# A four-layer transformer kernel: the second layer's bands, rotary tables and normalisation set in another order

## Chip, cores and metric

One core of one Trainium2 chip. The metric is the device time of one execution in microseconds. The kernel before took 1456.38 us, the median of three runs (1453.41 to 1458.69).

## What is computed

Eight blocks of 128 tokens by 512 values (x) pass through four layers of cross-attention and feed-forward; each sub-layer adds to x what it computes from the layer-normalised x. The change lies between the first feed-forward (L0F) and the second (L1F). The part of the reference that it touches:

```python
# L0 ffn: router softmax over 8 heads, low-rank A and B
scores = H * softmax(x @ Wr.T + br); low = einsum('bsd,hrd->bshr', x, A)
out = 2 * einsum('bshr,hor,bsh->bso', low, B, scores)
# L1 xattn: the 76 of 128 channels that are largest in the context are "crucial"
crucial, sub = mask * x, (1 - mask) * x
c = [max(crucial, ch), mean(crucial, ch)]; s = [max(sub, ch), mean(sub, ch)]
A1, A2 = (sigmoid(relu(batch_norm(conv1d(v, conv_w, pad=3)))) for v in (c, s))
x = x + crucial * A1 + sub * A2
# L1 ffn: top-2 router, low-rank pair, base product
x = x + ffn(layernorm(x))
# L3 xattn needs rotary tables: cos_t[position_ids], sin_t[position_ids]
# and k = ctx @ Wk (8 heads), v = ctx @ Wv
```

## The kernel before, in words

Every engine's work is written out by hand as one queue for each engine, in the functions under `block.sync` (SP, the loads and stores), `block.gpsimd` (POOL), `block.scalar` (ACT), `block.vector` (DVE) and the one of TensorE (PE); semaphores alone tie the queues together, so the order in which a queue is written is the order in which it waits. `link` (an instruction, then a wait of the same engine for it) is used where an engine reads what it has just written.

Float32 products run as three passes of a high and a low half (`mm3`, L413, L417, L418). Weights come in 137 units of 128x512: SP loads a unit into `stage` (5 places), ScalarE rounds it into `ring_h` (L1213), GpSimd writes the rest into `ring_l` (L1036), both rings have 10 places. `hi.upto(n)` and `lo.upto(n)` run these steps up to unit n, `load.upto(n)` the loads.

**Context pieces.** The keys and values of the fourth layer are 32 pieces of 12 products each (`kv_pe`, evicted by ScalarE in `kv_act`, L814, stored by SP). They depend on the context only and are strewn between other work as filler for TensorE. Piece i waits for the eviction of piece i - 2.

**Router 0** (`router_pe`, `router_act`, `router_dve` with i = 0). TensorE makes the logits and the low-rank product, turns the logits (L727), VectorE adds the bias and subtracts the maximum (L628 to L632), ScalarE takes exp (L600), VectorE weights `low` (L651); TensorE meanwhile runs pieces 0 to 3 and turns `low` (L755); VectorE multiplies (L658) and splits (L663). GpSimd at that time makes the low half of the context, `cTl` (L1084), 1024 wide.

**Masks loop** (L1690 to L1698). VectorE normalises the eight blocks into `xnf` (L464), TensorE transposes each (L2129), VectorE multiplies with the mask and takes maxima, ScalarE takes the sums (L1376). Transposes of block b wait for the masks of block b - 2. Pieces 6, 7 and 8 follow blocks 3, 5 and 7.

**Rotary tables.** For each quarter q of the tokens GpSimd writes a one-hot matrix of the positions (`one_hot`, L1093), TensorE multiplies the tables with it (`tables_pe`, L2117), ScalarE copies cosine and sine out (L1362). One-hot q waits for product q - 1. Quarter 0 is done before the masks loop, 1 to 3 after it, with pieces 9, 10 and 11 between.

**Bands and the chain** (L1699 to L1729). The convolution over channels is a product with six banded matrices, which VectorE builds from the 14 taps (`band`, L608 to L622: one shift matrix, then 6 chains of tensor_scalar and scalar_tensor_tensor) after the masks loop. TensorE then does 24 matmul records (L2144), VectorE, TensorE (two totals, L2148), GpSimd (square root, L1107, L1108) and ScalarE (exp, L1391) take turns, and VectorE has the gains. Piece 12 follows the totals.

**Factor loop** (L1731 to L1748). For each block VectorE makes the channel factors `gT` from mask and gains (L1737), TensorE transposes them (L2156), VectorE multiplies with `xnf` (L1746), adds to X (L1747) and takes statistics (`ln_step`, L432, L435). Pieces 13 to 17 follow blocks 1 to 5. After the loop the layer norm of L1F runs over all eight blocks: `ln_dve` (normalise L464, low half L479), `ln_pe` (transposes L497), `ln_act` (high half L517), with pieces 18 to 20; then router 1, whose low-rank product starts on TensorE at 390.23 us.

## Time and profile before

| | us |
|---|---|
| median of three runs | 1456.38 (1453.41 to 1458.69) |
| the profiled execution's own time | 1461.52 |
| its span, first to last instruction | 1459.7 |
| PE busy | 1322.6 (91%) |
| DVE busy | 959.1 (66%) |
| ACT busy | 594.0 (41%) |
| POOL busy | 548.5 (38%) |

A profile is one execution. Busy times of different engines overlap. The timeline gives, for each instruction or run of like ones (xN), its start from the span's start, the time it took, and in brackets how long the engine stood idle before it and what ended that. The windows view sums the same records over a stretch and adds the clock that TensorE was granted (1.00 is full speed, 0.50 half).

### The profile page before, as it was taken

The page shows a single profiled execution, that of the slowest core. Times are in us where ns is not written, and L with a number is a line of the kernel's source. Part 1 is how long each engine was busy: PE and PEld are TensorE (multiplying, and loading weights), DVE is VectorE, ACT ScalarE, POOL GpSimd, SP SyncE. Part 2 cuts the span into 40 slices and gives each one's busy share as a digit, 9 for nine tenths or more (in the row PEclk, how much of TensorE's full clock was granted, in tenths as well). Part 3 has the DMA queues.
Part 4 walks back from the last instruction along what each step waited for, and adds up shares of the span by engine and source line. Part 5 has one row for each costly group of instructions (what it writes and reads, how often), then busy time and mean ns, then how long its engine had stood idle before and what let it go on. Part 6 is the DMA issues. An engine that isn't in the chain of part 4 may idle for free.

```text
span 1459.7 us, 20660 instructions
## 1 busy us (share of the span) xinstructions
PE 1322.6 (91%) x6958; PEld 996.1 (68%) x6958; DVE 959.1 (66%) x2109; ACT 594.0 (41%) x1614; POOL 548.5 (38%) x548
## 2 busy tenths in 40 slices
PE   2888877988899999999999899999999999999797
PEld 1555544767677777677878777777777777777565
DVE  6999956596633688843222566777777777677745
ACT  2777773361312344433121324344343444344341
POOL 5001003642313444142221444464554645445274
PEclk9999887998999999999999999999999999999999
DMA  5211111211221000031110131011111111110001
GB/s 168 59 30 43 31 25 63 87 66 65 73 80 51 1 8 30 1 95 51 38 56 23 51 100 52 30 58 51 37 58 59 58 41 46 51 37 30 1 1 58
DMA packets 53610, 71.68 MB, mean 49 GB/s; under 512 B 5936, under 2 KB 24689, under 8 KB 53507
## 3 DMA queue, kind: packets, MB, share of 16 engines
q1 hardware_dynamic: 52592, 69.15, 15.0%
q10 hardware_dynamic: 914, 1.22, 0.3%
q8 instruction: 57, 0.93, 0.3%
q14 instruction: 47, 0.38, 0.1%
HBM read 55.67 MB, written 10.49 MB: 45 GB/s over the span
## 4 chain that ended last, share of the span: by engine, by line
PE 63%; DVE 17%; issue 7%; POOL 6%; ACT 4%; DMA 2%; SPq 1%; POOLq 0%; DVEq 0%; ACTq 0%
PE bank L413 15%; PE bank L418 14%; PE bank L417 14%; PE bank L2399 3%; DVE topv L1603 2%; PE bank L2279 2%; PE bank L2375 2%; POOL ring_l L1036 2%; PE bank L2261 2%; DVE top L1597 2%; PE bank L2386 1%; DVE bank L1883 1%; DVE xn L1863 1%; DVE xn L1849 1%; POOL probs L1183 1%
## 5 line engine op out<-in xcount | busy, mean ns | idle before, releaser
L1036 POOL TENSOR_TENSOR ring_l<-stage,ring_h 128x512 fp32r<-128x512 f32 x137 | 181.9, 1346 | 250.5 <-ACT ring_h L1213 250.5
L413 PE MATMUL bank<-xTh_b,ring_h 128*128 128x512 f32 x464 | 189.9, 409 | 4.4 <-issue 3.0
L417 PE MATMUL bank<-xTl_b,ring_h 128*128 128x512 f32 x464 | 184.3, 397 | 0.0
L418 PE MATMUL bank<-xTh_b,ring_l 128*128 128x512 f32 x464 | 184.3, 397 | 0.0
L1158 POOL TENSOR_TENSOR q<-xn 128x512 f32<-128x512 f32 x64 | 82.6, 1291 | 205.6 <-DVE xn L1863 205.6
L413 PE MATMUL bank<-ring_h,o3h 128*128 128x512 f32 x256 | 125.3, 490 | 3.5 <-issue 3.5
L1507 ACT ACTIVATE probsT<-bank 128x512 f32<-128x512 f32 x64 | 38.2, 598 | 203.4 <-PE bank L2386 203.4
L1519 ACT ACTIVATE probs<-bank,nbias 128x128 f32<-128x128 f32 x256 | 90.5, 366 | 51.0 <-DVE nbias L1885 51.0
L413 PEld LDWEIGHTS bank<-xTh_b,ring_h 128*128 128x128 f32 x464 | 88.0, 190 | 25.0 <-issue 6.4
L418 PEld LDWEIGHTS bank<-xTh_b,ring_l 128*128 128x128 f32 x464 | 87.7, 189 | 21.5
L418 PE MATMUL bank<-ring_h,o3l 128*128 128x512 f32 x256 | 101.6, 397 | 0.0
L417 PE MATMUL bank<-ring_l,o3h 128*128 128x512 f32 x256 | 100.6, 393 | 0.0
L417 PEld LDWEIGHTS bank<-xTl_b,ring_h 128*128 128x128 f32 x464 | 88.0, 190 | 18.3
L1863 DVE TENSOR_TENSOR xn<-bank,sinT 64x512 f32<-64x512 f32 x128 | 88.1, 688 | 1.7
L1213 ACT ACTIVATE ring_h<-stage 128x512 fp32r<-128x512 f32 x137 | 81.8, 630 | 17.2 <-DMA stage<-in_units_dram 16.9
L1895 DVE TENSOR_TENSOR o3l<-bank,o3h 128x512 fp32r<-128x512 f32 x64 | 44.3, 692 | 58.3 <-ACT o3h L1529 58.3
L1877 DVE TENSOR_TENSOR X<-X,bank 128x512 f32<-128x512 f32 x64 | 44.0, 687 | 52.2 <-PE bank L418 51.8
L1814 DVE TENSOR_TENSOR hid<-silu,bank 128x512 f32<-128x512 f32 x22 | 15.1, 688 | 93.9 <-PE bank L418 86.3
L2375 PEld LDWEIGHTS bank<-k,q 128*128 128x128 f32 x512 | 67.7, 193 | 7.0 <-issue 1.7
L1183 POOL TENSOR_TENSOR probs<-probs,rsums 128x512 f32<-128x512 f32 x64 | 66.6, 1040 | 15.4 <-DVE rsums L1891 15.4
L2399 PE MATMUL bank<-probsT,v 128*128 128x512 f32 x128 | 67.2, 606 | 4.8 <-ACT probsT L1507 4.8
L2375 PE MATMUL bank<-k,q 128*128 128x128 f32 x512 | 68.3, 277 | 0.3 <-POOL q L1158 0.3
(332 smaller groups left out, 3249.4 us busy)
## 6 DMA issues: line engine op xcount, KB each, us to landing
stage<-in_units_dram SPq DMA_DIRECT2D x137, 256.0 KB, 3.0
ring_l<-k SPq DMA_DIRECT2D x64, 64.0 KB, 2.1
raw_k<-kvs SPq DMA_DIRECT2D x16, 256.0 KB, 2.1
kraw<-raw_k SPq DMA_DIRECT2D x16, 256.0 KB, 3.5
v<-raw_v SPq DMA_DIRECT2D x16, 256.0 KB, 2.8
stage<-in_context_dram SPq DMA_DIRECT2D x8, 256.0 KB, 2.9
raw_v<-kvs SPq DMA_DIRECT2D x8, 256.0 KB, 2.0
out_dram<-X SPq DMA_DIRECT2D x8, 256.0 KB, 2.0
```

The source lines that it names most:

```text
L413: ins = nc.tensor.matmul(out_ap, wh, mh, start=start, stop=False)
L417: nc.tensor.matmul(out_ap, wh, ml, start=False, stop=False)
L418: return nc.tensor.matmul(out_ap, wl, mh, start=False, stop=stop)
L1036: nc.gpsimd.tensor_tensor(ring_l[:, place_of(u), :], stage[:, u % STAGE, :], f32(ring_h[:, place_of(u), :]), ALU.subtract).then_inc(w_lo, 1)
L1158: nc.gpsimd.tensor_tensor(dst, xn[:, (at - 1) % 2, :], xn[:, 2 + (at - 1) % 2, :], ALU.add).then_inc(a3_ad, 1)
L1183: nc.gpsimd.tensor_tensor(pb, pb, rsums[:, n % 4, :].unsqueeze(2).to_broadcast((P, 4, P)), ALU.mult).then_inc(a3_pn, 1)
L1213: nc.scalar.activation(ring_h[:, place_of(u), :], stage[:, u % STAGE, :], ACT.Copy).then_inc(w_hi, 1)
L1519: ins = nc.scalar.activation(probs[:, n % 3, c], bank[n % 2][:, c], ACT.Exp, bias=nbias[:, n % 4, r:r + 1], scale=-1.0, accum_out=psums[:, ...
L1863: ins = nc.vector.tensor_tensor(xn[to, 2 + i % 2, :], src[fro, :], sinT[to, c], ALU.mult)
L1895: nc.vector.tensor_tensor(o3l[:, m % 2, :], bank[3 + m % 2][:], f32(o3h[:, m % 2, :]), ALU.subtract).then_inc(a3_ol, 1)
L2375: ins = nc.tensor.matmul(bank[n % 2][:, r * P:(r + 1) * P], q3[:, r, c], k3[:, c], start=True, stop=True)
L2399: nc.tensor.matmul(bank[3 + m % 2][:], v3[:, m % 8, :], probsT[:, m % 3, :], start=True, stop=True).then_inc(a3_pv, 1)
```

## The change

- `band` for the bands 0 to 2 is called in `router_dve` (i = 0) ahead of the wait for the turned logits, for 3 to 5 behind the weighting of `low`; the call after the masks loop goes.
- Rotary tables: cosine and sine (64 rows each) are one 128-row table, so a quarter's product has half the matmuls. `tables_pe(1)` moves behind block 1's transposes in the masks loop, `tables_pe(2)` behind block 5's, `tables_pe(3)` behind piece 9. ScalarE copies per half of the tokens, four copies of 64 rows each, the first half of the sine negated, after its sums.
- Pieces 6, 7 and 8 follow blocks 2, 4 and 6 of the masks loop; pieces 10 and 11 the two totals; 12 to 17 blocks 2 to 7 of the factor loop; 18 to 20 come after it. Pieces 12 to 17 use banks 4 and 5 instead of 6 and 7; piece 12 waits for ScalarE's second table copy.
- The layer norm of L1F is made block by block in the factor loop: statistics at once (`ln_one`), normalising one round later, transposes after the piece of round b + 2, the low half three rounds later. GpSimd takes the square roots in `ln_root`, with the low parts of units 12 and 13 between.
- GpSimd's one-hot 2 comes before unit 8's low part. SP loads one unit further ahead from piece 8 on.
- `xnf` is multiplied in place, `gT` lies in `probs` and `probsT`, both totals in one bank. VectorE still makes the channel factors, four instructions a block.

In the order of the file (the tables' constants and the buffers are left out):

```diff
-        tabs = probsT[:, 0:2, :].rearrange("p a (k j) -> p a k j", k=KT)
+        tabs = probsT[:, 0, :].rearrange("p (k j) -> p k j", k=KT)
+        gT = (probs[:, 2, :], probsT[:, 2, :])
...
+            if i == 0:
+                for k in range(3):
+                    band(v, k)
...
+            if i == 0:
+                for k in range(3, 6):
+                    band(v, k)
...
+                if i == 12:
+                    t.wait_ge(su_rc, 2)
...
-        def router_pe(t, i, n_ln, u, th, tl):
-
-            def between(b):
-
-                if b == 3:
-                    kv_pe(t, 21)
-                if b == 5:
-                    router_logits_pe(t, i, 0, th, tl)
-
-            if i == 1:
-                kv_pe(t, 20)
-                ln_pe(t, n_ln, between)
+        def router_pe(t, i, u, th, tl):
+
-            if i == 1:
-                t.wait_ge(c_ev, 21)
...
-            first = 0 if i < 4 else 6 if i < 18 else 4 if i < 24 else 0
+            first = 0 if i < 4 else 6 if i < 12 else 4 if i < 24 else 0
...
-            nc.sync.dma_start(tabs, d["tabs"].rearrange("a k p j -> p a k j")).then_inc(s_rest, 16)
+            nc.sync.dma_start(tabs, d["tabs"].rearrange("k p j -> p k j")).then_inc(s_rest, 16)
-                load.upto(unit_kv(i) + (10 if i >= 18 else 5))
+                load.upto(unit_kv(i) + (10 if i >= 18 else 6 if i >= 8 else 5))
...
+            one_hot(2)
-            one_hot(2)
-            lo.upto(U_L1F)
-            ln_pool(g, LN_L1F[0])
+            lo.upto(12)
+            for b in range(B):
+                ln_root(g, LN_L1F[0], b)
+                if b < 2:
+                    lo.upto(13 + b)
...
-            def tables(q):
-
-                a.wait_ge(su_rope, q + 1)
-                for i in range(2):
-                    ins = nc.scalar.activation((cosT, sinT)[i][:, q * 256:(q + 1) * 256], bank[5 - 3 * (q % 2)][:, i * 256:(i + 1) * 256],
-                                               ACT.Copy)
-                ins.then_inc(su_rc, 1)
-
-            tables(0)
+            def tables(half):
+
+                a.wait_ge(su_rope, 2 * half + 2)
+                c = slice(half * HALF, (half + 1) * HALF)
+                low_rows, high_rows = slice(0, 64), slice(64, P)
+                for to in (low_rows, high_rows):
+                    nc.scalar.activation(cosT[to, c], bank[5 - half][low_rows, :], ACT.Copy)
+                nc.scalar.activation(sinT[low_rows, c], bank[5 - half][high_rows, :], ACT.Copy, scale=-1.0)
+                nc.scalar.activation(sinT[high_rows, c], bank[5 - half][high_rows, :], ACT.Copy).then_inc(su_rc, 1)
+
...
-                if b in (3, 5, 7):
-                    kv_act(a, 6 + (b - 1) // 2)
-                if b in (4, 6):
-                    hi.upto(7 + b // 2)
+                if b in (2, 4, 6):
+                    kv_act(a, 6 + b // 2)
+                if b in (3, 5):
+                    hi.upto(9 + b // 5)
+            kv_act(a, 10)
+            tables(0)
-            kv_act(a, 10)
-            tables(2)
-            kv_act(a, 11)
-            tables(3)
-            kv_act(a, 12)
-            hi.upto(11)
+            hi.upto(12)
-            kv_act(a, 13)
-            hi.upto(12)
-            kv_act(a, 15)
-            hi.upto(U_L1F)
-            kv_act(a, 18)
+            kv_act(a, 12)
+            for b in range(B):
+                if b < 2:
+                    hi.upto(13 + b)
+                else:
+                    kv_act(a, 11 + b)
+                    ln_act(a, LN_L1F[1], xTh_a, b - 1, b - 2)
+            kv_act(a, 19)
+            ln_act(a, LN_L1F[1], xTh_a, 7, 6)
+            hi.upto(U_L1F + 1)
+            kv_act(a, 20)
+            ln_act(a, LN_L1F[1], xTh_a, 8, 7)
-            kv_act(a, 20)
-            ln_act(a, LN_L1F[1], xTh_a, 4)
-            ln_act(a, LN_L1F[1], xTh_a, 8, 4)
...
-            for i in range(6):
-                band(v, i)
...
-            nc.vector.tensor_copy(zs[:, 3, :], bank[4][:, 0:2]).then_inc(x_rows, 1)
+            nc.vector.tensor_copy(zs[:, 3, :], bank[3][:, 2:4]).then_inc(x_rows, 1)
...
-            link(v, v_chain, nc.vector.tensor_tensor(gains[:, 2, :], gains[:, 0, :], gains[:, 1, :], ALU.subtract))
+            nc.vector.tensor_tensor(gains[:, 2, :], gains[:, 0, :], gains[:, 1, :], ALU.subtract).then_inc(x_rows, 1)
+                else:
+                    v.wait_ge(x_rows, 4)
-                    ins = nc.vector.tensor_scalar(gT[:, b % 2, q * P:(q + 1) * P], crucial[:, i, :], gains[:, 2, i:i + 1],
+                    ins = nc.vector.tensor_scalar(gT[b % 2][:, q * P:(q + 1) * P], crucial[:, i, :], gains[:, 2, i:i + 1],
-            for b in range(B):
-                if b + 1 < B:
-                    gains_by_channel(b + 1)
-                v.wait_ge(x_gp, b + 1)
-                link(v, v_chain, nc.vector.tensor_tensor(tmpx[:, b % 2, :], bank[b % 2][:], xnf[:, b, :], ALU.mult))
-                nc.vector.tensor_tensor(X[:, b, :], X[:, b, :], tmpx[:, b % 2, :], ALU.add).then_inc(x_done, 1)
-                ln_step(v, LN_L1F[0], b)
-            ln_step(v, LN_L1F[0], B)
-            ln_step(v, LN_L1F[0], B + 1)
-
-            ln_dve(v, *LN_L1F, xTh_a, xTl_a)
+            for b in range(B + 3):
+                if b < B:
+                    if b + 1 < B:
+                        gains_by_channel(b + 1)
+                    v.wait_ge(x_gp, b + 1)
+                    link(v, v_chain, nc.vector.tensor_tensor(xnf[:, b, :], bank[b % 2][:], xnf[:, b, :], ALU.mult))
+                    nc.vector.tensor_tensor(X[:, b, :], X[:, b, :], xnf[:, b, :], ALU.add).then_inc(x_done, 1)
+                    ln_one(v, LN_L1F[0], b)
+                if 1 <= b <= B:
+                    ln_row(v, *LN_L1F, b - 1)
+                if b >= 3:
+                    ln_low(v, LN_L1F[1], b - 3, xTh_a, xTl_a)
...
-            router_pe(t, 0, LN_L0F[1], U_L0F, xTh_a, xTl_a)
+            router_pe(t, 0, U_L0F, xTh_a, xTl_a)
...
-                if q >= 2:
-                    t.wait_ge(su_rc, q - 1)
-                for i in range(2):
-                    for k in range(KT):
-                        ins = nc.tensor.matmul(bank[5 - 3 * (q % 2)][:, i * 256:(i + 1) * 256], tabs[:, i, k, :], hot[:, k, :],
-                                               start=k == 0, stop=k == KT - 1)
+                for k in range(KT):
+                    ins = nc.tensor.matmul(bank[5 - q // 2][:, q % 2 * 256:(q % 2 + 1) * 256], tabs[:, k, :], hot[:, k, :],
+                                           start=k == 0, stop=k == KT - 1)
...
-                if b in (3, 5, 7):
-                    kv_pe(t, 6 + (b - 1) // 2)
-            tables_pe(1)
+                if b == 1:
+                    tables_pe(1)
+                if b in (2, 4, 6):
+                    kv_pe(t, 6 + b // 2)
+                if b == 5:
+                    tables_pe(2)
-            tables_pe(2)
-            kv_pe(t, 11)
-            kv_pe(t, 12)
-            t.wait_ge(su_rc, 4)
...
-                nc.tensor.matmul(bank[3 + j][:, 0:2], ones_f[:, :], zs[:, 1 + j, :], start=True, stop=True).then_inc(x_tot, 1)
-            kv_pe(t, 13)
+                nc.tensor.matmul(bank[3][:, 2 * j:2 * j + 2], ones_f[:, :], zs[:, 1 + j, :], start=True, stop=True).then_inc(x_tot, 1)
+            kv_pe(t, 12)
-                    ins = nc.tensor.transpose(bank[b % 2][:, c], gT[:, b % 2, c], ident[:, :])
+                    ins = nc.tensor.transpose(bank[b % 2][:, c], gT[b % 2][:, c], ident[:, :])
-                if 1 <= b <= 5:
-                    kv_pe(t, 13 + b)
-
-            t.wait_ge(c_ev, 18)
-            router_pe(t, 1, LN_L1F[1], U_L1F, xTh_a, xTl_a)
+                if b >= 2:
+                    kv_pe(t, 11 + b)
+                    if b == 2:
+                        t.wait_ge(c_ev, 12)
+                    ln_turn(t, LN_L1F[1], b - 2)
+            kv_pe(t, 19)
+            ln_turn(t, LN_L1F[1], 6)
+            t.wait_ge(x_done, XD_L1X + 7)
+            router_logits_pe(t, 1, 0, xTh_a, xTl_a)
+            kv_pe(t, 20)
+            ln_turn(t, LN_L1F[1], 7)
+            kv_pe(t, 21)
+            router_logits_pe(t, 1, 1, xTh_a, xTl_a)
+            t.wait_ge(c_ev, 21)
+            router_low_pe(t, 1, 0, U_L1F, xTh_a, xTl_a)
+            router_turn_logits_pe(t, 1)
+            router_low_pe(t, 1, 1, U_L1F, xTh_a, xTl_a)

```

## Rows read from the trace of the kernel before

**Rows 1.** The page, part 1: busy us (share of the span), instructions.

```profile
PE 1322.6 (91%) x6958; PEld 996.1 (68%) x6958; DVE 959.1 (66%) x2109; ACT 594.0 (41%) x1614; POOL 548.5 (38%) x548
```

**Rows 2.** Windows: stretch, length, busy us of PE, PEld, DVE, ACT, POOL; clock; DMA.

```profile
295.60:316.70 21.10, 16.88 (x75) 13.91 (x76) 20.55 (x34) 19.12 (x119) 6.10 (x6) 0.84 0.18 62
...
335.00:346.80 11.80, 8.99 (x42) 7.21 (x40) 6.02 (x22) 2.02 (x5) 2.16 (x3) 0.71 0.14 44
346.80:368.00 21.20, 18.93 (x88) 15.23 (x88) 20.62 (x50) 5.01 (x9) 6.86 (x10) 0.92 0.25 87
368.00:390.20 22.20, 18.33 (x96) 12.84 (x97) 14.37 (x28) 7.12 (x13) 6.47 (x11) 1.00 0.32 107
390.20:446.00 55.80, 53.97 (x229) 40.44 (x228) 20.51 (x64) 8.92 (x16) 15.08 (x23) 1.00 0.16 52
```

**Rows 3.** Timeline of VectorE, router 0: start, us, engine, line, operation, idle before.

```profile
253.24 1.29 DVE L479 TENSOR_TENSOR xTl_a<-bank,xTh_a 128x512 fp32r<-128x512 f32 x2 [3.39 <-ACT xTh_a L517]
...
261.11 0.23 DVE L628 TENSOR_TENSOR lg<-bank,br 128x64 f32<-128x64 f32 x1 [6.58 <-PE bank L727]
...
261.63 4.80 DVE L632 TENSOR_TENSOR lg<-lg,rt 128x64 f32<-128x64 f32 x1
...
277.09 1.29 DVE L658 SCALAR_TENSOR_TENSOR lows<-bank,lows 128x512 f32<-128x512 f32 x2 [8.56 <-PE bank L755]
```

**Rows 4.** Timeline of VectorE: the first and last instruction round the bands.

```profile
316.68 0.48 DVE L612 TENSOR_SCALAR probs<-iota,con 128x512 f32<-128x512 f32 x1
...
327.81 0.45 DVE L1703 TENSOR_SCALAR rows<-rows 128x32 f32<-128x32 f32 x2
```

**Rows 5.** Timeline of GpSimd, router 0.

```profile
255.54 2.43 POOL L1084 TENSOR_TENSOR cTl<-probs,cTh 128x1024 fp32r<-128x1024 f32 x1
...
262.65 2.45 POOL L1084 TENSOR_TENSOR cTl<-sinT,cTh 128x1024 fp32r<-128x1024 f32 x1
265.03 1.31 POOL L1036 TENSOR_TENSOR ring_l<-stage,ring_h 128x512 fp32r<-128x512 f32 x1
```

**Rows 6.** Timeline of ScalarE: evictions of context pieces 0, 1 and 8.

```profile
268.25 0.60 ACT L814 ACTIVATE kvs<-bank 128x512 f32<-128x512 f32 x1 [1.05 <-PE bank L418]
271.05 0.60 ACT L814 ACTIVATE kvs<-bank 128x512 f32<-128x512 f32 x1 [2.20 <-PE bank L418]
...
318.65 0.58 ACT L814 ACTIVATE kvs<-bank 128x512 f32<-128x512 f32 x1
```

**Rows 7.** Timeline of TensorE: a tables product, the next piece, the band matmuls.

```profile
313.59 3.62 PE L2117 MATMUL bank<-hot,probsT 128*128 128x256 f32 x16
316.85 0.58 PE L413 MATMUL bank<-cTh,ring_h 128*128 128x512 f32 x1
...
334.99 2.76 PE L2144 MATMUL bank<-rows,bands 128*128 128x32 f32 x24
```

**Rows 8.** Timeline of GpSimd: the second one-hot.

```profile
296.77 3.63 POOL L1093 TENSOR_SCALAR hot<-probs,con 128x256 f32<-128x256 int32 x4
```

**Rows 9.** Timeline of VectorE: the masks of blocks 0 and 2.

```profile
295.58 0.68 DVE L1694 TENSOR_TENSOR cf<-bank,crucial 128x512 f32<-128x512 f32 x1
...
300.85 0.68 DVE L1694 TENSOR_TENSOR cf<-bank,crucial 128x512 f32<-128x512 f32 x1
```

**Rows 10.** Timeline of TensorE: second total, first factor transposes (one piece lies between).

```profile
340.31 0.59 PE L2148 MATMUL bank<-zs,ones_f 128*128 128x2 f32 x2 [1.39 <-DVE zs L1717]
...
346.76 0.66 PE L2156 MATMUL bank<-ident,gT 128*128 128x128 f32 x4 [0.64 <-DVE gT L1737]
```

**Rows 11.** Timeline of VectorE: two groups of factors in the factor loop.

```profile
352.97 1.10 DVE L1737 TENSOR_SCALAR gT<-crucial,gains 128x128 f32<-128x128 bf16 x4
...
359.57 2.42 DVE L1737 TENSOR_SCALAR gT<-crucial,gains 128x128 f32<-128x128 bf16 x4
```

**Rows 12.** Timeline of VectorE: additions of two successive blocks in the first layer.

```profile
241.94 0.68 DVE L1675 TENSOR_TENSOR X<-X,bank 128x512 f32<-128x512 f32 x1
...
244.55 0.68 DVE L1675 TENSOR_TENSOR X<-X,bank 128x512 f32<-128x512 f32 x1
```

More of the change, by code:

```diff
@@ L79, in constants @@
     inv = (1.0 / np.float32(10000.0) ** (np.arange(0, P, 2, dtype=np.float32) / np.float32(P))).astype(np.float32)
-    ang = np.concatenate([t * inv, t * inv], 1).astype(np.float32)
-    sin = np.sin(ang)
-    sin[:, :64] *= -1
-    tabs = np.stack([np.cos(ang), sin]).astype(np.float32).reshape(2, KT, P, P)
+    ang = (t * inv).astype(np.float32)
+    tabs = np.concatenate([np.cos(ang), np.sin(ang)], 1).astype(np.float32).reshape(KT, P, P)
     rep = np.zeros((P, 8, P), np.float32)
@@ L300, in program @@
         ex = ExitStack()
-        xnf = sb("xnf", [P, B, D], F32, ex)
         cf = sb("cf", [P, 2, 2, 512], F32, ex)
+        junk = sb("junk", [P, 2, 4, P], F32, ex)
         rows = sb("rows", [P, 2, 2, B, 6], F32, ex)
-        junk = sb("junk", [P, 2, 4, P], F32, ex)
         z = sb("z", [P, 2, 32], F32, ex)
@@ L307, in program @@
         zs = sb("zs", [P, 8, 2], F32, ex)
+        ones_f = sb("ones_f", [P, P], F32, ex)
+        under_low = sb("under_low", [P, 2 * KT * TOK - 2 * 4 * P - 2 * 2 * 512 - 4 * B * 6 - 2 * 64 - 16 - P], F32, ex)
+        xnf = sb("xnf", [P, B, D], F32, ex)
         gains = sb("gains", [P, 3, 32], F32, ex)
-        gT = sb("gT", [P, 2, 512], F32, ex)
-        tmpx = sb("tmpx", [P, 2, 512], F32, ex)
-        ones_f = sb("ones_f", [P, P], F32, ex)
         ex.close()
```

## The prediction

> **What bounds the kernel now.** I read the page first: TensorE is busy 1322.6 of 1459.7 us [rows 1], so work taken from another engine counts only where TensorE waits for it. Then I cut the stretch that the diff touches into windows [rows 2]; look there at TensorE's busy time beside the length, and at the granted clock. In the masks loop (295.6 to 316.7) VectorE is busy 20.55 of 21.1 us, TensorE 16.88 at a clock of 0.84. From 335 to 346.8 (band convolution, batch-norm chain) TensorE is busy 8.99 of 11.8 at 0.71; a 0.71 is a mixture of its two levels, 1.2 and 2.4 GHz. In the factor loop and the normalisation it idles 2.3 and 3.9 us. From 390.2 on it is busy 53.97 of 55.8 at full clock, and what follows hangs on it. So the time changes by what happens to one date: the start of the second router's low-rank product on TensorE, 390.2 now. I follow that date through five marks.
>
> **Mark 1, router 0.** Three bands go in front of VectorE's wait for the logits. VectorE is free from 254.53 (253.24 + 1.29) to 261.11 [rows 3]. All six bands now run from 316.68 to 327.81 [rows 4], 11.1 us; bands 0 to 2 are 16 instructions in 5.9 us of that, bands 3 to 5 the other 5.2. By length both halves fit, the second into the 8.56 us before 277.09 [rows 3]. But GpSimd runs tensor_tensor without a gap from before 255.54 to 266.34 (last start 265.03 + 1.31) [rows 5], and a 64-wide VectorE operation with two SBUF inputs that starts at 261.63 takes 4.80 us: it ends at 266.43, 0.09 after GpSimd's stream [rows 3]. A band is a chain of scalar_tensor_tensor with two SBUF inputs. Read as that row reads, all 16 wait until 266.34 and end at 272.2. The Trainium skill (SBUF — State Buffer, section "Who interferes with whom") says that such an instruction and a reading GpSimd one exclude each other for one whole instruction; by that, VectorE gets one in after each GpSimd instruction, and the bands would end near 270. The trace agrees that they exclude each other, but its 4.80 us row passed the ends of two GpSimd instructions (near 262.7 and 265.1) without getting in.
>
> Then follow subtract (0.75 us with its two predecessors), exp on ScalarE, the `lows` copy, and the eviction of context piece 0, now at 268.25 [rows 6]. TensorE's third piece waits for that eviction; pieces take 2.80 each (268.25 to 271.05, [rows 6]), so TensorE is there at 270.75. With bands ending at 270, it starts 1.6 late; with 272.2, 3.5 late. Bands 3 to 5 then end as late (278.5 to 280.4 against 277.09), beside the two late pieces, not behind them. Ends of the range: 1.5, and 5 if the 3.5 us pause also costs a stretch at half clock. I take **+3.0**, nearer to the row than to a free boundary.
>
> **Mark 2, masks loop.** The tables' product now has 8 records where it had 16: it took 3.26 us (313.59 to 316.85) [rows 7], now 1.63; four of them save 6.5 us of TensorE. But product 1 moves from behind the loop to behind block 1's transposes, where it waits for GpSimd's one-hot 1, finished at 300.40 (296.77 + 3.63) [rows 8]. Queued behind that wait are block 2's transposes, which VectorE wants at 300.85 [rows 9]. TensorE waits there some 6 us; after shorter pauses the clock was at half in this same stretch [rows 2], so the product takes up to 3 us. One-hot 1 at 303.1 (+3.0, -0.3 as ScalarE reaches its unit earlier), product until 304.7 to 306.1, transposes 0.5 to 0.8: VectorE is ready at 303.9 and stalls 1.5 to 3.2. Behind come piece 6 (2.8 to 3.5 us) and only then block 3's transposes: 0 to 1.5 more. I take 3.5 in all (ends 1.5 and 6). The loop ends at 316.7 + 3.0 + 3.5 = 323.2. One-hots 2 and 3, also later in their order on GpSimd, have 7 us and more before products 2 and 3.
>
> **Mark 3, band matmuls**, at 334.99 [rows 7]. The 11.1 us of bands after the loop go, as do TensorE's pieces 10 and 11 ahead of them. What is late next is ScalarE: it ended its sums and began its next eviction at 318.65, 2.0 after the loop [rows 6]. So 323.2 + 2.0, scaling 0.5, 0.1 to TensorE: **325.8, that is -9.2**. Piece 9 and the last tables' product end near 324.
>
> **Mark 4, first factor transposes.** From 334.99 to 346.76 the chain takes 11.8 us [rows 7, 10]. VectorE's part stays. TensorE now has two pieces after the second total (340.31 [rows 10], 5.3 after the bands) where it had one, which took 5.3 us at half clock until the pause before 346.76: 5.6 to 8.4 us for both, so +11.4 to +14.1. GpSimd has two low parts ready behind its square root instead of one, and can hold VectorE's next step once more, 0 to 1.2. I take +12.6: **338.4, -8.4**.
>
> **Mark 5, the factor loop with the normalisation in it.** VectorE's factors stay (1.10 us a block [rows 11]), and each round now also holds statistics, normalising and the low half. This very pattern runs in the layer before: 2.61 us a round with the addition (241.94 to 244.55) [rows 12], its waits on itself included. Plus 0.7 for the product with `xnf` (0.68 for the like in [rows 9]) and 1.10 for the factors: 4.4. TensorE has 0.4 + 2.8 + 0.4 = 3.6 in a round, so VectorE bounds the loop. Round 0 is 2.3, rounds 1 and 2 are 3.85 (no low half yet), rounds 3 to 5 are 4.43 (the sum unrounded), then factors 7: from mark 4, 1.0 + 2.3 + 7.7 + 13.3 + 1.2 = 25.5. Then TensorE alone: factor transposes 0.4, four pieces 11.2, three normalised blocks 1.3, two halves of logits 5.6, 18.5 in all. GpSimd's low parts fall into the loop as before: a factor group took 2.42 instead of 1.10 at 359.57 [rows 11]; I allow that once and 0.9 for a second, 2.2 together. 338.4 + 46.2 = 384.6 against 390.2: **-5.6**. In short: the loop with normalisation takes 46.2 where it took 43.4, because nine pieces instead of eight lie there and VectorE's work per round is longer than TensorE's.
>
> **Costed at nothing.** The half-size tables' DMA and the unit loaded one step ahead: the first lies under the router, and unit 13, whose load now waits in SP's queue for piece 11's eviction, is wanted by ScalarE some 3 us after it, by TensorE only at piece 16, and the square root behind its low part in GpSimd's queue two rounds later. ScalarE's table copies grow to eight of at most 0.60: they lie between its sums and the exp, which waits for most of the 11.8 us chain. The wait `su_rc` before piece 12 is 10 us old by then. The other buffers (xnf in place, factors in `probs`/`probsT`, totals in one bank) have no later readers. If ScalarE's cover went, up to 4.8 us would show at the exp.
>
> Sum: **-5.5 us**. It is made against the profiled execution, 1461.52, so 1456.0; that one is 5.1 above the median of the three, 1456.38, which I use: **1450.9**. A measurement of this kernel tells some 0.3% (4.4 us) from no change.
>
> **Rivals.** *Waits eat it (0.25).* Mark 1 costs 5, mark 2 costs 5.5: +4 on the sum, halved where marks 4 and 5 take up slack, gives -3.5 to -1.5, about 1453.9. For it: the 4.80 row, and clock 0.84 in the masks loop. Against it: mark 1's pause is short.
> *More comes off (0.12).* Bands slip in between GpSimd's instructions, transposes of block 2 come on time: -10.5, 1445.9. For it: the length fits. Against it: one-hot 1 ends at 300.4 whatever VectorE does.
> *Slower, by the clock in the factor loop (0.11).* TensorE now pauses 0.8 us in each round. At half clock a piece takes 5.3 [rows 10] and a round 6 to 6.6, some 2.2 above VectorE's 4.43. From 2.5 such rounds the gain is gone; five cost 11 us: +5.5, 1461.9. For it: the clock was 0.92 from 346.8 to 368 [rows 2]. Against it: it was 1.00 from 368 to 390.2 with TensorE busy 18.33 of 22.2, more idle than I expect of the loop (3.6 of 4.43).
> *It doesn't do what it says:* if the bands' first half waits out the stream completely, only bands 3 to 5 are hidden; that is the first rival.
>
> **Numbers.** My forecast has 0.52, within -7.5 to -3.5; four fifths of it lie beyond 0.3%. Faster 0.42 + 0.12 = 0.54; same 0.10 + 0.24 = 0.34; slower 0.12. The range takes in the first two rivals: 1444 to 1457.5, which leaves out the slower case and the far tail.
>
> **What would show it.** Right: VectorE's first bands start near 254.5 with durations far over 0.4 us and end between 270 and 272; TensorE idles before its third piece; a wait of about 6 us of the tables' product for the one-hot; band matmuls near 326; rounds of 4.4 us in the factor loop with TensorE idle 0.8; low-rank product near 384.6. Wrong: bands of normal length before 261; masks rounds of 2.64 throughout; a clock under 0.9 in the factor loop; or a new wait after 384.6.

## The result and the profile after

The changed kernel takes 1454.24 us (median of 20 runs, 1449.77 to 1456.71), the kernel before in as many runs of the same comparison 1458.36. The ratio is 0.9972, with a 95% interval of 0.9962 to 0.9982: 4.1 us off, between 2.6 and 5.5. Forecast were 5.5 off and 1450.9. The measured time lies in the range of 1444 to 1457.5. The gain is 0.28%, just under the 0.3% that the prediction took as the bound of "faster", so by its own bound the outcome is "same", which it gave 0.34, and not "faster", which it gave 0.54. Of the 3.3 us between 1450.9 and 1454.24, 2.0 are the base: the kernel before has 1458.36 as the median of 20 runs, where the prediction had three runs with 1456.38.

The page's part 1 after the change, beside [rows 1]:

```profile
PE 1315.2 (91%) x6926; PEld 990.7 (68%) x6926; DVE 965.0 (66%) x2109; ACT 595.9 (41%) x1614; POOL 548.9 (38%) x548
```

TensorE is busy 7.4 us less, in 32 records fewer: the four tables products have eight fewer each. VectorE is busy 5.9 us more with the same number of instructions: some of them take longer beside GpSimd's, as the timelines below show. The profiled execution took 1454.35 us (span 1452.5), that of before 1461.52, so the two profiles lie 7.2 apart, the medians 4.1. The profiled run of the kernel before is 3.2 above its median, and 1.0 of the 7.2 is there before the change begins (254.53 against 253.52 for the instant that the table below counts from). What follows finds the time of one execution, and the medians say how much of it stays.

The windows of the changed kernel, with the columns of [rows 2]:

```profile
296.90:322.00 25.10, 20.91 (x96) 17.06 (x96) 20.79 (x33) 20.54 (x126) 13.35 (x14) 0.93 0.16 54
325.00:337.00 12.00, 9.83 (x37) 8.49 (x37) 5.73 (x17) 5.24 (x10) 3.40 (x4) 0.60 0.09 26
337.00:364.40 27.40, 22.46 (x116) 16.99 (x114) 26.76 (x65) 7.16 (x13) 8.12 (x14) 1.00 0.25 87
364.40:383.20 18.80, 18.78 (x89) 12.78 (x90) 8.95 (x16) 5.88 (x11) 4.55 (x6) 1.00 0.36 126
383.20:439.00 55.80, 53.97 (x229) 40.48 (x228) 20.52 (x64) 8.93 (x16) 15.12 (x23) 1.00 0.16 52
```

Read the last line first. The 55.8 us after the second router's low-rank product are the ones of before, 53.97 of TensorE in both, so that product's date is still what counts; it is 383.16 where it was 390.23. In the factor loop (337.0 to 364.4) VectorE is busy 26.76 of 27.4 and TensorE at full clock; behind it TensorE is busy 18.78 of 18.8. The band convolution's chain (325 to 337) ran at a clock of 0.60, worse than the 0.71 of before; from the first band matmul to the first factor transposes it is 0.66 (323.47 to 338.43).

The date of the whole stretch moves by a microsecond or two from run to run before the change begins. So I set every mark against one instant ahead of it: the end of the last two low halves of the first feed-forward's norm on VectorE (253.24 + 1.29 in [rows 3]; 252.23 + 1.29 after). In a3, b1 and c1 two bands lie ahead of that instant; it still comes after a wait for ScalarE there, of 1.0 to 1.1 us. The table, in us from that instant, is worked out from the timelines of each profile; the "rest" is from the low-rank product to the end of the span.

| kernel | y products of router 0 | first masks | masks end | band matmuls | first factor transposes | low-rank product | rest |
|---|---|---|---|---|---|---|---|
| before | 24.79 | 41.05 | 62.24 | 80.46 | 92.23 | 135.70 | 1069.50 |
| after | 25.99 | 43.35 | 67.61 | 69.95 | 84.91 | 129.64 | 1069.39 |
| c2, before with the bands moved | 26.00 | 42.87 | 64.07 | 82.15 | 93.72 | 138.20 | 1063.74 |
| a1, after with the bands back | 24.78 | 41.86 | 66.91 | 77.33 | 94.10 | 138.85 | 1066.44 |
| a2, tables product 1 later | 26.00 | 43.08 | 64.25 | 66.78 | 81.68 | 126.42 | 1063.44 |
| b4, the same once more | 26.01 | 43.35 | 65.33 | 67.06 | 80.87 | 125.62 | 1066.28 |
| a3, bands outside GpSimd's stream | 24.92 | 42.01 | 66.97 | 69.30 | 84.24 | 128.98 | 1069.92 |
| a4, layer norm behind the loop | 26.00 | 43.36 | 67.74 | 70.08 | 85.05 | 132.25 | 1066.45 |
| b1, a2 with a3 | 24.92 | 42.02 | 63.21 | 65.72 | 80.65 | 125.40 | 1069.76 |
| b2, factors on ScalarE | 26.01 | 43.36 | 67.63 | 69.97 | 85.20 | 126.05 | 1069.70 |
| b3, a2 with b2 | 25.99 | 43.35 | 65.22 | 67.06 | 80.82 | 122.86 | 1072.34 |
| c1, a2 with a3 and b2 | 24.92 | 42.04 | 63.22 | 65.75 | 80.67 | 122.65 | 1069.31 |

**Router 0.** VectorE's timeline after, answering to [rows 3]; L610, L617 and L619 are the bands:

```profile
253.44 1.42 DVE L610 TENSOR_SCALAR probs<-iota,con 128x512 f32<-128x512 f32 x1
254.89 2.34 DVE L617 TENSOR_SCALAR bands<-probs,conv 128x128 f32<-128x128 f32 x1
257.26 4.83 DVE L619 SCALAR_TENSOR_TENSOR bands<-probs,conv,bands 128x128 f32<-128x128 f32 x2
...
262.13 2.32 DVE L617 TENSOR_SCALAR bands<-probs,conv 128x128 f32<-128x128 f32 x1
264.48 3.21 DVE L619 SCALAR_TENSOR_TENSOR bands<-probs,conv,bands 128x128 f32<-128x128 f32 x6
267.73 0.29 DVE L617 TENSOR_SCALAR bands<-probs,conv 128x128 f32<-128x128 f32 x1
268.05 0.74 DVE L619 SCALAR_TENSOR_TENSOR bands<-probs,conv,bands 128x128 f32<-128x128 f32 x2
268.82 0.22 DVE L629 TENSOR_TENSOR lg<-bank,br 128x64 f32<-128x64 f32 x1
...
277.28 1.29 DVE L662 SCALAR_TENSOR_TENSOR lows<-bank,lows 128x512 f32<-128x512 f32 x2 [0.90 <-PE bank L749]
```

and GpSimd's of the same stretch:

```profile
254.53 2.60 POOL L1078 TENSOR_TENSOR cTl<-probs,cTh 128x1024 fp32r<-128x1024 f32 x1
257.10 2.42 POOL L1078 TENSOR_TENSOR cTl<-probsT,cTh 128x1024 fp32r<-128x1024 f32 x1
259.49 2.46 POOL L1078 TENSOR_TENSOR cTl<-cosT,cTh 128x1024 fp32r<-128x1024 f32 x1
261.91 2.46 POOL L1078 TENSOR_TENSOR cTl<-sinT,cTh 128x1024 fp32r<-128x1024 f32 x1
264.33 1.28 POOL L1030 TENSOR_TENSOR ring_l<-stage,ring_h 128x512 fp32r<-128x512 f32 x1
```

Lay the two over each other: a VectorE instruction begins and then lasts until just after the next GpSimd one has begun (254.89 + 2.34 = 257.23 beside 257.10; 257.26 + 4.83 = 262.09, two instructions, beside 259.49 and 261.91; 262.13 + 2.32 = 264.45 beside 264.33). One of VectorE's gets in for each of GpSimd's. From 266 on all run at 0.3 to 0.4 us, and the bands are done at 268.8. On TensorE's timeline the third context piece and, behind it, the y products:

```profile
270.88 0.50 PE L411 MATMUL bank<-cTh,ring_h 128*128 128x512 f32 x1 [0.60 <-ACT kvs L808]
...
279.51 0.47 PE L411 MATMUL bank<-ring_h,lowT_h 128*128 128x512 f32 x1 [1.89 <-DVE lowT_l L667]
...
280.57 0.63 PE L411 MATMUL bank<-ring_h,lowT_h 128*128 128x512 f32 x1
```

The piece waits 0.60 us, and the y products run at half clock (0.63 us) until 283.1.

**The masks loop.** TensorE's timeline, where the tables' product 1 now stands, then product 2 and the band matmuls:

```profile
300.51 3.62 PE L2114 MATMUL bank<-hot,probsT 128*128 128x256 f32 x8 [5.46 <-POOL hot L1087]
303.96 0.60 PE L2126 MATMUL bank<-ident,xnf 128*128 128x128 f32 x4
...
311.32 1.89 PE L2114 MATMUL bank<-hot,probsT 128*128 128x256 f32 x8
...
323.47 4.59 PE L2140 MATMUL bank<-rows,bands 128*128 128x32 f32 x24 [2.05 <-DVE rows L1700]
...
330.81 0.59 PE L2144 MATMUL bank<-zs,ones_f 128*128 128x2 f32 x2 [1.39 <-DVE zs L1714]
...
338.43 0.60 PE L2152 MATMUL bank<-ident,probs 128*128 128x128 f32 x4
```

The product waits 5.46 us for its one-hot and then takes 3.62 us for eight matmuls, where product 2 takes 1.89 for as many: half clock. Block 2's transposes stand behind both. VectorE's timeline shows what that costs:

```profile
304.60 0.69 DVE L1693 TENSOR_TENSOR cf<-bank,crucial 128x512 f32<-128x512 f32 x1 [2.38 <-PE bank L2126]
...
307.84 0.69 DVE L1693 TENSOR_TENSOR cf<-bank,crucial 128x512 f32<-128x512 f32 x1 [0.51 <-PE bank L2126]
...
323.15 0.27 DVE L1700 TENSOR_SCALAR rows<-rows 128x32 f32<-128x32 f32 x2 [2.02 <-ACT junk L1374]
```

**The factor loop.** Four additions to X in VectorE's timeline, with the two places where it takes longer beside GpSimd's low parts, the first addition and a group of factors:

```profile
343.07 1.07 DVE L1747 TENSOR_TENSOR X<-X,xnf 128x512 f32<-128x512 f32 x1
...
345.45 2.08 DVE L1736 TENSOR_SCALAR probsT<-crucial,gains 128x128 f32<-128x128 bf16 x4
...
351.90 0.69 DVE L1747 TENSOR_TENSOR X<-X,xnf 128x512 f32<-128x512 f32 x1
...
356.25 0.69 DVE L1747 TENSOR_TENSOR X<-X,xnf 128x512 f32<-128x512 f32 x1
...
360.59 0.69 DVE L1747 TENSOR_TENSOR X<-X,xnf 128x512 f32<-128x512 f32 x1
```

A round takes 4.35 us.

### The profile page after: what moved, and what is told of

Read it like the earlier page. It is cut to its first block, busy times and chain, and to the rows that moved or that the text cites. A ratio compares the mean times of both kernels' runs of the same rounds, so it can differ in the third digit from the quotient of the medians.

```text
span 1452.5 us, 20595 instructions
## 1 busy us (share of the span) xinstructions
PE 1315.2 (91%) x6926; PEld 990.7 (68%) x6926; DVE 965.0 (66%) x2109; ACT 595.9 (41%) x1614; POOL 548.9 (38%) x548
## 4 chain that ended last, share of the span: by engine, by line
PE 62%; DVE 19%; issue 6%; POOL 5%; ACT 5%; DMA 2%; SPq 1%; POOLq 0%; DVEq 0%; ACTq 0%
PE bank L411 15%; PE bank L415 14%; PE bank L416 14%; PE bank L2407 3%; DVE topv L1602 2%; PE bank L2287 2%; PE bank L2383 2%; PE bank L2269 2%; POOL ring_l L1030 2%; DVE top L1596 2%; PE bank L2394 1%; DVE bank L1883 1%; DVE xn L1863 1%; DVE xn L1849 1%; PE bank L495 1%
## 5 line engine op out<-in xcount | busy, mean ns | idle before, releaser
L1180 POOL TENSOR_TENSOR probs<-probs,rsums 128x512 f32<-128x512 f32 x64 | 66.6, 1040 | 15.9 <-DVE rsums L1891 15.9
```

Of the source, the lines that this page charges most:

```text
L1180: nc.gpsimd.tensor_tensor(pb, pb, rsums[:, n % 4, :].unsqueeze(2).to_broadcast((P, 4, P)), ALU.mult).then_inc(a3_pn, 1)
```

## The experiments

Each was timed beside the kernel before; these comparisons were four (the change; a1 to a4; b1 to b4; c1 and c2), and the kernel before had medians from 1458.36 to 1460.65 us in them, so versions of different comparisons are compared by their ratios. The profiled runs of c2 and a2 are not typical: c2's took 1457.08 us, 4.7 under its median, and a2's 1446.18 is the fastest of its six. Medians and ratios:

| kernel | us | ratio (95% interval) |
|---|---|---|
| a1 | 1461.66 | 1.0026 (1.0006 to 1.0047) |
| c2 | 1461.78 | 1.0006 (0.9988 to 1.0023) |
| a4 | 1454.98 | 0.9983 (0.9965 to 1.0001) |
| a3 | 1452.77 | 0.9971 (0.9950 to 0.9992) |
| b2 | 1450.4 | 0.9947 (0.9929 to 0.9966) |
| b4 | 1449.97 | 0.9940 (0.9926 to 0.9954) |
| b1 | 1448.79 | 0.9937 (0.9922 to 0.9951) |
| b3 | 1449.42 | 0.9934 (0.9918 to 0.9950) |
| a2 | 1447.18 | 0.9928 (0.9909 to 0.9947) |
| c1 | 1447.36 | 0.9917 (0.9895 to 0.9938) |

### a1: the bands back behind the masks loop

```diff
-            if i == 0:
-                for k in range(3):
-                    band(v, k)
...
+            for i in range(6):
+                band(v, i)
             v.wait_ge(x_sum, B)
```

> The changed kernel with all six bands made after the masks loop again, as before; tables, pieces and normalisation stay as changed. Theory A (the date of the second router's low-rank product decides, part by part): the 11 us of bands come back after the loop, of which ScalarE's sums covered 2.0; router 0 gets back the 2.7 us that its late bands cost. So some 6 us slower than the changed kernel (4 to 8): 1460, ratio to the kernel before near 1.001. Rival B (the gain is only the tables' saved TensorE work, whatever the order): within 1 us of the changed kernel, ratio 0.997. Rival C (it hangs on where the half-clock stretches fall): same as B, but with three or more stretches of half clock fewer or more between 250 and 360 us.

Measured: 1461.66 us, ratio 1.0026 where the change has 0.9972, some 7 to 8 us slower than the changed kernel, at the upper end of the 4 to 8 expected. The band matmuls in TensorE's timeline:

```profile
331.83 5.33 PE L2136 MATMUL bank<-rows,bands 128*128 128x32 f32 x24 [10.12 <-DVE rows L1696]
```

TensorE stands idle 10.12 us for VectorE, and then runs at half clock. At the low-rank product this version is 9.2 us behind the changed kernel (138.85 against 129.64). With the rest of the change in place, the bands' new place is worth more than the whole gain. The order that stays costs a1 something of its own: its tables product waits 6.72 us for the one-hot, and the masks loop ends at 66.91, 4.7 us later than in the kernel before.

### c2: the same part alone, in the kernel before

The diff is that of the change for `router_dve` and for the call behind the loop; nothing else is touched.

> The kernel before with one part of the change alone: the bands in the router's two waits. Theory A: in the kernel before TensorE had its own queue until the band matmuls (from 313.59 to 334.99 it stood idle 2.1 us in all, for one-hots), so the bands off VectorE free nobody; what remains is the 1.2 us by which the y products come later. Band matmuls at 80.5 to 82 us after the low halves, second low-rank product at 135.5 to 137, time 1458 to 1460, ratio 0.999 to 1.003; VectorE has a new idle time of about 9 us before the chain. Theory B (bands on VectorE were the bound by themselves): band matmuls 7 to 9 us earlier, near 72, ratio near 0.995.

Measured: ratio 1.0006, no difference. The chain's first step on VectorE, the band matmuls and the tables product ahead of them on TensorE:

```profile
338.30 0.22 DVE L1711 COPY z<-bank 128x64 f32<-128x64 f32 x1 [18.45 <-PE bank L2148]
```

```profile
321.64 3.72 PE L2121 MATMUL bank<-hot,probsT 128*128 128x256 f32 x16 [0.99 <-POOL hot L1099]
...
329.14 3.72 PE L2121 MATMUL bank<-hot,probsT 128*128 128x256 f32 x16 [0.98 <-POOL hot L1099]
...
335.50 2.76 PE L2148 MATMUL bank<-rows,bands 128*128 128x32 f32 x24
```

VectorE scales the rows 7.2 us earlier from the common instant (319.43 - 253.35, where it was 327.81 - 254.53 [rows 4]) and then idles 18.45: TensorE comes to the band matmuls without a wait in front of them, straight from pieces 9 to 11 and the tables products between. They start 1.7 us later than before, not 7 to 9 earlier, so theory B falls. Together a1 and c2 say that two queues meet at the band matmuls. In the kernel before VectorE was through at 327.81 + 0.45 [rows 4] and TensorE at 334.99 [rows 7], 6.7 later. Freeing the earlier one alone gives nothing (c2). Freeing the later one alone (a1) brings the band matmuls to 10.4 us behind the end of the masks loop, where before and c2 have 18.2 and 18.1 and the change has 2.3. So TensorE's part alone is worth 7.8 us there. Of these, 4.7 are lost by the later end of the loop, which leaves 3.1, and the chain behind, at a clock of 0.58, takes 16.8 us instead of 11.8 and loses the rest. That a1 gains nothing in the time is thus no property of the join; a version of a1 with the tables product later was not run. The change frees both: the bands on VectorE, and on TensorE pieces 10 and 11, the tables' placement and their half size. What pieces, placement and half size are worth each was not measured. In c2 the low-rank product came 2.5 us later (138.20), outside the 135.5 to 137 expected: the loop began 1.8 late, and the stretches at half clock fell otherwise.

### a2 and b4: the tables' product 1 behind block 3's transposes

```diff
-                if b == 1:
-                    tables_pe(1)
                 if b in (2, 4, 6):
                     kv_pe(t, 6 + b // 2)
+                if b == 3:
+                    tables_pe(1)
```

> The changed kernel with the second tables product behind block 3's transposes instead of block 1's. Theory A: TensorE no longer waits 5.5 us for one-hot 1, block 2's transposes come on time, VectorE's stalls in the masks loop (2.4 and 0.5 us) go: 2 to 3 us faster than the changed kernel, ratio near 0.995. Rival B: no difference, since TensorE's work is the same. Rival C: as A only where the clock of the loop changes with it.

> The late-table kernel once more, for a second profile. It was 7 us faster than the changed kernel, but the low-rank product started only 3.2 us earlier; what came after it took 1063.4 instead of 1069.4 us, with fewer stretches at half clock. Theory A: the further 6 us are where those stretches fall, so they need not be there again: 1447 again only if the profile shows the same two stretches missing after the low-rank product; otherwise 1451. Rival (the order change itself saves work later): the rest is 1063.4 again with the same clock as in the changed kernel.

Measured: 0.9928 and, repeated, 0.9940, both better than the 0.9972 of the change with intervals that don't meet. In TensorE's timeline of a2 the product no longer waits for the one-hot, and runs at full clock:

```profile
299.13 0.63 PE L2126 MATMUL bank<-ident,xnf 128*128 128x128 f32 x4 [4.61 <-DVE cf L1694]
303.94 0.60 PE L2126 MATMUL bank<-ident,xnf 128*128 128x128 f32 x4
304.38 1.89 PE L2114 MATMUL bank<-hot,probsT 128*128 128x256 f32 x8
```

TensorE still waits here, 4.61 us, but for VectorE, which keeps its pace of one block in 2.64 us: what the change lost was not TensorE's waiting but block 2's transposes behind it. The low-rank product comes 3.2 and 4.0 us earlier. By the ratios the time came down by 0.44% and 0.32%, 6 and 5 us, where 2 to 3 had been expected of a2; in the profiles the part that is over lies in the rest (1063.4 and 1066.3 against 1069.4), which no edit touched. b4 was to show whether a2's short rest belongs to the order: it does not. The same program has the two stretches at half clock, 75 and 235 us behind the low-rank product, that a2 lacks and the changed kernel has.

### a3: only band 1 in GpSimd's stream

```diff
             if i == 0:
-                for k in range(3):
-                    band(v, k)
+                band(v, 1)
...
+                if i == 10:
+                    v.wait_ge(s_rest, 64)
+                    band(v, 0)
+                    band(v, 2)
                 if i >= 4:
                     ln_low(v, LN_L0F[1], i - 4, xTh_a, xTl_a)
```

> The changed kernel with the shift matrix and bands 0 and 2 made before the low half of block 6 of the first feed-forward's normalisation, in the 3.4 us in which both VectorE and GpSimd stand idle; only band 1 stays ahead of the router's wait. Theory A (bands 0 to 2 wait for GpSimd's port, one instruction for each of GpSimd's): the bands end about 3 us earlier, TensorE's third piece is on time and the half-clock stretch at the low-rank output goes: 2 to 3 us faster than the changed kernel, ratio near 0.9955. Rival B: no difference. If the port is held only by the first instructions, under 1 us.

Measured: ratio 0.9971, the same as the change. The router came 1.1 us earlier, and of that 0.66 arrived at the low-rank product. VectorE's timeline:

```profile
248.04 0.74 DVE L619 SCALAR_TENSOR_TENSOR bands<-probs,conv,bands 128x128 f32<-128x128 f32 x2
...
253.28 11.38 DVE L619 SCALAR_TENSOR_TENSOR bands<-probs,conv,bands 128x128 f32<-128x128 f32 x6
264.69 0.23 DVE L628 TENSOR_TENSOR lg<-bank,br 128x64 f32<-128x64 f32 x1
```

The same instruction takes 0.37 us before the stream and 1.9 inside it. The gain of 1.1 us is the delay that the change has there, and the 2 to 3 us expected in the time did not come. The first masks are 1.3 us earlier, the end of the loop 0.6: the wait for the one-hot takes the other 0.7 back. In b1, where that wait is gone, the loop ends 1.0 to 2.1 earlier than in a2 and b4.

### a4: the layer norm behind the factor loop

```diff
-                    ln_one(v, LN_L1F[0], b)
-                if 1 <= b <= B:
-                    ln_row(v, *LN_L1F, b - 1)
-                if b >= 3:
-                    ln_low(v, LN_L1F[1], b - 3, xTh_a, xTl_a)
+                    ln_step(v, LN_L1F[0], b)
+            ln_step(v, LN_L1F[0], B)
+            ln_step(v, LN_L1F[0], B + 1)
+            ln_dve(v, *LN_L1F, xTh_a, xTl_a)
```

with the other queues in the order of before.

> The changed kernel with the layer norm after the factor loop, all eight blocks, as before; bands, tables and the pieces' places in the loop stay as changed. Theory A (VectorE bounds the streamed loop, so that streaming brings little): the stretch from the first factor transposes to the low-rank product goes from 44.7 to 44.5 to 48 us: 0 to 3 us slower than the changed kernel, ratio 0.997 to 0.999. Rival (streaming carries the gain): 5 us slower or more, ratio over 1.000.

Measured: ratio 0.9983. From the first factor transposes to the low-rank product it takes 47.2 us (132.25 - 85.05) against 44.7. At that mark the streamed norm is worth 2.6; in the time the ratios differ by 0.1% with intervals that overlap, so there it is not shown.

### b2: the channel factors on ScalarE

```diff
-                    ins = nc.vector.tensor_scalar(gT[b % 2][:, q * P:(q + 1) * P], crucial[:, i, :], gains[:, 2, i:i + 1],
-                                                  gains[:, 1, i:i + 1], ALU.mult, ALU.add)
+                    ins = nc.scalar.activation(gT[b % 2][:, q * P:(q + 1) * P], crucial[:, i, :], ACT.Identity,
+                                               scale=gains[:, 2, i:i + 1], bias=gains[:, 1, i:i + 1])
```

> The changed kernel with the channel factors made by ScalarE (Identity with scale and bias per partition) instead of VectorE. Theory A (VectorE's 4.36 us a round bound the factor loop): a round falls to TensorE's 3.6 to 3.7 us, the stretch from the first factor transposes to the low-rank product from 44.7 to about 40.5 us, the time to 1450. Rival (TensorE bounds it all the same, by its pieces and waits for ScalarE): 44.7 stays within 1 us, 1454.

Measured: 1450.4 us, ratio 0.9947. Three factor transposes in TensorE's timeline:

```profile
349.88 0.60 PE L2156 MATMUL bank<-ident,probs 128*128 128x128 f32 x4
353.56 0.60 PE L2156 MATMUL bank<-ident,probsT 128*128 128x128 f32 x4
357.23 0.60 PE L2156 MATMUL bank<-ident,probs 128*128 128x128 f32 x4
```

They stand 3.67 apart, with no wait ahead of them: a round is now TensorE's 3.6, and from the first transposes to the low-rank product it takes 40.85 us (126.05 - 85.20) instead of 44.7. VectorE's factors did bound the loop. In the time the gain over the change is 0.25%, with intervals that just overlap (0.9929 to 0.9966 and 0.9962 to 0.9982).

### b1, b3 and c1: the parts together

b1 is a2 with a3's edit, b3 is a2 with b2's, c1 all three.

> The changed kernel with the second tables product behind block 3 and bands 0 and 2 in the quiet 3.4 us. The band order alone gave 1.1 us at the low-rank output, of which 0.4 was left at the end of the masks loop, since block 2's transposes waited for the one-hot either way. Theory A: with that wait gone the whole 1.1 to 1.4 us arrives: the masks loop ends 62.9 to 63.3 after the reference instant (64.25 with the late table alone), the low-rank product starts near 125.1 (126.4), the time falls 1 to 1.5 us below the late table's, 1446. Rival (the two overlap in something else, or the half-clock stretches move): no gain on 1447.2.

> The late tables product and ScalarE's factors together. Theory A (the two costs lie one behind the other): their gains add, low-rank product near 122.3 after the reference instant, 1443. Rival (freed time is lost in half-clock stretches, as VectorE gets idle and TensorE's pauses move): 1446 or more.

> The kernel after with the second quarter's tables product behind block 3's transposes, only band 1 in the first router wait, and the channel factors on ScalarE. Second low-rank product at 122.0 to 122.9 us after the low halves (122.86 with two of the three). If the stretches at half clock in the rest stay as in the kernel after (rest 1069.5): 1446 to 1447. If the rest takes longer again when TensorE comes earlier, as in the version with two of the three (1072.3): 1449 to 1450, no better than the tables product alone.

Measured: 0.9937, 0.9934 and 0.9917. Each comes to the low-rank product within 0.6 us of what was expected, at 125.40, 122.86 and 122.65. The time doesn't follow: b3 is 2.8 us ahead of b4 there and ends no sooner. Its rest is longer by 6 us. Against b4 its half-clock time is longer in two places, 485 to 495 and 965 to 1000 us after the low-rank product. The windows view of the second, 970 to 1000 us after it, first the changed kernel, then b3:

```profile
1353.16:1383.16 30.00, 22.22 (x106) 16.37 (x106) 19.98 (x39) 10.81 (x24) 5.56 (x10) 0.94 0.00 1
```

```profile
1346.18:1376.18 30.00, 22.13 (x86) 16.56 (x86) 18.65 (x36) 9.13 (x21) 5.03 (x9) 0.83 0.00 1
```

A third place, which sets a2 apart from the changed kernel, is 70 to 85 us after that product: a2 has no half-clock stretch there. The changed kernel, then a2:

```profile
453.16:468.16 15.00, 13.21 (x51) 10.23 (x50) 3.75 (x7) 5.58 (x11) 6.23 (x5) 0.89 0.32 87
```

```profile
450.93:465.93 15.00, 13.20 (x57) 10.35 (x56) 4.34 (x7) 5.51 (x11) 6.24 (x5) 1.00 0.28 88
```

These clocks go with the rests of 1072, 1069 and 1063 us. Over the twelve profiles the half-clock time in the rest, added up from windows of 5 us, goes from 10 to 27 us, and the rests from 1063.4 to 1072.3 follow it roughly. The whole rest in the windows view, first of a2, then of b3:

```profile
380.93:1444.40 1063.47, 1015.45 (x5245) 787.90 (x5243) 656.72 (x1039) 384.71 (x1064) 448.71 (x417) 0.99 0.14 43
```

```profile
376.18:1448.50 1072.32, 1022.67 (x5245) 793.37 (x5243) 656.80 (x1039) 384.79 (x1064) 448.31 (x417) 0.99 0.14 43
```

The number of records is the same, and VectorE, ScalarE and GpSimd are busy as long in both to within 0.4 us. Of the 8.9 us, 7.2 are matmuls of TensorE that take longer, the other 1.6 its idle time. So the longer rest is in the main TensorE's own clock. What sets where the stretches fall is open: each profile is one execution, and a2 and b4, the same program, differ by 2.8 us. c1 has the lowest ratio, 0.9917, some 12 us below the kernel before; its interval overlaps with those of a2, b1, b3 and b4, so it is not shown to beat them. All five beat both the kernel before and the change.

## Why the prediction was right, and where its steps were off

The prediction counts on the axis of its own profile, on which every instant after the change is 1.01 us later than the rows above say (254.53 against 253.52).

**Mark 1, +3.0: measured +1.2.** The step that was off is "nearer to the row than to a free boundary". Read as the 4.80 us row reads, the bands end at 272.2; they ended at 268.79, which is 269.8 on the prediction's axis. The Trainium skill's rule (SBUF — State Buffer, section "Who interferes with whom"), one instruction excluded for one whole instruction of the other engine, is what the two timelines above show: one in for each of GpSimd's. It was worked out to 270, and that was right. (The bands 0 to 2 with the shift matrix are 14 instructions, not the 16 that the prediction counts; their 5.9 us are right.) The third piece waited 0.60 us for the eviction and began 1.1 late, where 1.6 to 3.5 were expected. For this case the prediction allowed a stretch at half clock only in the upper end of its range, and it came: TensorE's matmuls of the y products ran at half clock from 280.14 to 283.13 (0.63 instead of 0.39 us each). The normalisation for the masks begins 2.2 late (292.08 against 290.88 on the two axes) and the first masks 2.3 late. The stretch is 1.0 of the 2.2: in a2, where it did not come, the normalisation begins 1.2 late. But a2's first masks are still 2.0 late, since the last two normalising instructions take 1.99 us there beside a low part of GpSimd, where they took 1.17 before; so little of the first masks' delay hangs on the clock.

**Mark 2, +6.5: measured +5.4.** The stalls were 2.38 + 0.51 = 2.9, where 3.5 had been taken from a range of 1.5 to 6 (the terms that the prediction names add up to 4.7, not 6). The mechanism is as it was written: a wait of 5.46 us (some 6 expected), a product of 3.62 (up to 3 expected), the transposes behind. a2 and b4 removed it and won, by the date, 3.2 and 4.0.

**Mark 3, -9.2: measured -10.5.** The lag behind the loop, ScalarE's sums, was 2.02 us with 2.0 expected; 1.1 of the 1.3 us of delay forecast too much come from marks 1 and 2. c2 and a1 show that this term belongs to two parts at once. The prediction took both away in one sentence and gave no price for either alone; with the bands' part alone the term would have been none (c2), with TensorE's alone about half of the 15.9 us (7.8 in a1).

**Mark 4, -8.4: measured -7.3.** This is the mis-sized term: +12.6 expected from the band matmuls to the first transposes, out of 11.4 to 14.1 and up to 1.2 more for a hold by GpSimd, and 15.0 measured. "5.3 after the bands" for the second total was the full-clock number of before. The matmuls now come after a wait of 2.05 us, most of them run at half clock (4.59 us instead of 2.76 [rows 7]), and the second total is 7.3 behind their start. From there to the first transposes, with the two pieces between, it is 7.6, within the 5.6 to 8.4 for the pieces. The second hold by GpSimd came too, 1.43 us for a pair that takes 0.51 in c2. It cost nothing more, since the two pieces filled TensorE's time up to the transposes.

**Mark 5, -5.6: measured -6.1.** The loop with the norm took 44.7 us, 46.2 expected; a round 4.35 with 4.43 expected. Both holds beside GpSimd's low parts appeared (1.07 instead of 0.69, 2.08 instead of 1.11), in sum 1.4 and not 2.2. That VectorE bounds the loop is shown by b2.

**The sum.** At the low-rank product the forecast was right within 0.5 us, and part of that is luck, since errors of 1 to 2 us cancel: 1.3 too much delay up to the band matmuls, 2.4 too little in the chain, 1.5 too much in the loop. By the medians 4.1 of the 6.1 arrived. What is missing isn't found in these two profiles, whose rests are the same within 0.1. The rests of the twelve differ by up to 9 us, which is more than what is missing; where it went stays open.

**The rivals.** *Waits eat it* named 1453.9, and the time is 1454.24, but that is chance: the base was 2.0 too low, the gain of 4.1 lies outside the 1.5 to 3.5 of this rival, and marks 1 and 2 cost 2.3 (at the first masks) and 2.9, not 5 and 5.5. *Slower by the clock in the factor loop* falls: the clock there was 1.00, with TensorE idle 4.9 of 27.4 us. *More comes off* asked for transposes of block 2 on time, and a2 and b4, which have them, took 10.5 and 8.8 us off (0.72% and 0.60%), with 10.5 named; that the first agrees so well is chance, as the same program gave both. No new wait came after 384.6: the first 55.8 us and the whole rest took as long as before.

## What to carry to other kernels

Before moving work off an engine, ask of each queue that meets at the next join when it would be through by itself. Here two were 6.7 us apart: relieving the earlier one alone gave nothing (c2), relieving the later one alone gave about half (7.8 of 15.9 us at the join in a1, lost again elsewhere), and both together gave the whole. A filler that waits for another engine doesn't fill, and what stands behind it in the queue pays: the tables product waited 5.5 us, ran at half clock and held up the transposes that VectorE wanted; two blocks further down it waited for nothing and ran at full clock. And carry the clock into a chain that starts with a wait, since a duration read at full clock was no price for the same matmuls after a wait of 2.05 us: 2.76 us became 4.59.

## What had not been expected of the hardware

- The same pause did not always bring half clock. The y products start after 1.89 us of idle time in the changed kernel and after 1.83 in the one before; in the first their matmuls take 0.63 us, in the second 0.39. The 0.60 us before the third piece look like the difference: the five profiles without it (before, a1, a3, b1, c1) have full clock there, and six of the seven with it have half clock. The seventh is a2, with waits of 0.59 and 1.89 us and full clock, and b4, the same program, has half clock; so the waits alone do not decide it. In the factor loops of the change and of b2, with waits of 0.3 to 2.6 us in the first rounds, the clock was 1.00.
- A 128-wide scalar_tensor_tensor takes 0.37 us alone and 1.9 to 2.4 in GpSimd's stream of 1024-wide operations. A tensor_scalar with one tensor as input in SBUF is held as well: 2.34 instead of 0.29 us.
- The subtraction of 4.80 us of before [rows 3] stays unexplained: the bands in the same stream were held for one GpSimd instruction each.
- Same program, other time far away: a2 and b4 agree within 0.8 us at the low-rank product, and their rests differ by 2.8.
